# Retained values made with tokens on partitions, scores as weights, in a rearranged token stage

## What is computed

```python
Q = split_heads(x @ Wq); K = split_heads(x @ Wk); V = split_heads(x @ Wv)
G = jax.nn.swish(x @ Wg + bg)
Dmask = gammas[:, None, None] ** jnp.maximum(diff, 0.0) * causal
scores = jnp.einsum('bhtd,bhsd->bhts', Q, K) / scale
ret = jnp.einsum('bhts,bhsd->bhtd', scores * Dmask[None], V)
ret = ret.transpose(0, 2, 1, 3).reshape(B, T, D)
ln = (ret - mu) / jnp.sqrt(var + LN_EPS) * ln_gamma + ln_beta
return ln * G @ Wo + bo
```

## Time and profile before

| | before |
|---|---|
| median of 3 runs | 776.42 us (776.38 to 776.57) |
| profiled execution, its own time | 773.9 us |
| its span (first to last instruction) | 772.1 us |
| PE busy, PEld busy | 741.4, 608.0 us |
| DVE, ACT, POOL busy | 408.4, 325.5, 184.0 us |
| token stage, from the first q product to the end | from 515.4 us |

### The profile page before, as it was taken

The page is one execution under the profiler, slowest core; times in us unless marked ns, Lnnn a source line. Parts: engine busy times, 40 slices in busy tenths (PEclk is TensorE's granted clock), DMA queues, the critical chain, the costliest instruction groups (busy, mean ns, idle before and its releaser), DMA issues.

```text
span 772.1 us, 18699 instructions
## 1 busy us (share of the span) xinstructions
PE 741.4 (96%) x7464; PEld 608.0 (79%) x7464; DVE 408.4 (53%) x1100; ACT 325.5 (42%) x698; POOL 184.0 (24%) x150
## 2 busy tenths in 40 slices
PE   3999999999999999999999999999999999999985
PEld 2778888888888888988888888778777777777742
DVE  6433333334655534453523333494588788778685
ACT  2436555463353434444344445542343343343232
POOL 1510000003975664754600000011110110110010
PEclk9999999999999999999999999999999999999999
DMA  7141334331322123022121115260000000000001
GB/s 257 70 175 61 112 116 139 111 106 68 115 86 89 58 85 116 31 85 61 31 61 31 33 60 203 73 232 1 1 1 14 14 0 14 14 0 14 0 1 41
DMA packets 33956, 53.63 MB, mean 69 GB/s; under 512 B 2416, under 2 KB 23152, under 8 KB 32656
## 3 DMA queue, kind: packets, MB, share of 16 engines
q1 hardware_dynamic: 29168, 36.05, 14.1%
q0 software_dynamic: 3328, 16.78, 6.1%
q10 hardware_dynamic: 1440, 0.53, 0.3%
HBM read 51.19 MB, written 2.16 MB: 69 GB/s over the span
## 4 chain that ended last, share of the span: by engine, by line
PE 94%; DVE 4%; ACT 1%; issue 1%; DMA 1%; POOL 0%; DVEq 0%; POOLq 0%
PE bank L227 68%; PE bank L550 4%; PE bank L395 4%; PE bank L566 4%; PE bank L409 3%; PE bank L515 3%; PE bank L386 3%; PE bank L503 2%; PE bank L491 1%; PE bank L559 1%; DMA X<-in_x 1%; PE bank L465 1%; PE bank L522 0%; DVE h_max L1221 0%; PE bank L354 0%
## 5 line engine op out<-in xcount | busy, mean ns | idle before, releaser
L227 PE MATMUL bank<-ctx_high,wk_high 128*128 128x258 f32 x512 | 147.6, 288 | 0.0
L227 PE MATMUL bank<-ctx_low,wk_high 128*128 128x258 f32 x512 | 144.8, 283 | 0.0
L227 PE MATMUL bank<-ctx_high,wk_low 128*128 128x258 f32 x512 | 144.3, 282 | 0.0
L227 PEld LDWEIGHTS bank<-ctx_high,wk_high 128*128 128x128 f32 x512 | 96.9, 189 | 13.6 <-issue 13.3
L227 PE MATMUL bank<-wv_high,ctx_high 128*128 128x512 f32 x256 | 106.0, 414 | 0.0
L227 PE MATMUL bank<-wv_low,ctx_high 128*128 128x512 f32 x256 | 101.3, 396 | 0.0
L227 PE MATMUL bank<-wv_high,ctx_low 128*128 128x512 f32 x256 | 100.9, 394 | 0.0
L687 ACT ACTIVATE vals<-bank 128x512 f32<-128x512 f32 x64 | 38.2, 597 | 144.3 <-PE bank L227 144.3
L227 PEld LDWEIGHTS bank<-ctx_low,wk_high 128*128 128x128 f32 x512 | 96.8, 189 | 0.0
L227 PEld LDWEIGHTS bank<-ctx_high,wk_low 128*128 128x128 f32 x512 | 96.6, 189 | 0.0
L677 ACT ACTIVATE kT<-bank,bxk 128x257 f32<-128x257 f32 x128 | 60.1, 470 | 57.4 <-PE bank L227 57.2
(11 more groups left out here) (200 smaller groups left out, 1409.4 us busy)
## 6 DMA issues: line engine op xcount, KB each, us to landing
raw<-in_ctx_t SPq DMA_DIRECT2D x32, 514.0 KB, 4.0
stage<-in_w POOLq DMA_DIRECT2D x16, 1024.0 KB, 5.9
X<-in_x SPq DMA_DIRECT2D x4, 512.0 KB, 7.2
v_last<-last_values SPq DMA_DIRECT2D x32, 64.0 KB
out<-X SPq DMA_DIRECT2D x8, 256.0 KB, 2.0
stage<-in_w_xq SPq DMA_DIRECT2D x1, 1024.0 KB, 8.1
stage<-in_w_xk SPq DMA_DIRECT2D x1, 1024.0 KB, 13.2
stage<-in_w_xv SPq DMA_DIRECT2D x1, 1024.0 KB, 5.6
```

What stands on the lines that cost most here:

```text
L227: last = pe.matmul(to, left(i, c), right(j, c), start=(c == 0 and i + j == 0), stop=(c == C - 1 and i == 1))
```

## The change

`retain` swaps its operands: the decayed scores (128 rows, 128 columns) are the weights, the head's values are 32 moving columns, and the result has tokens on the partitions, as the normalisation wants it. `turn_retained`, ScalarE's copy into `rT_sb` and the tile itself are gone. `retention_scores` runs with g outside and j inside, and stands ahead of `feed_down`; it waits for the v product's copy and for `keep_hidden` at its start. TensorE waits for all four decays before the first half of `feed_up`, and `retain` comes behind that half. On VectorE `add_retained` and the moments of y come ahead of the scaling of the next tokens, `gate(t)` comes behind the whole of `quantise_tokens`, and `decay_scores` ahead of `add_forward` and `finish_gate`. On GpSimd the deviation of y comes ahead of `add_bias`.

```diff
-            def retention_scores(t):
+            def retention_scores(t, down, more):
 
                 pe.wait_ge(tqT_kept, t + 1)
                 pe.wait_ge(tkT_kept, t + 1)
-                for j in range(HG):
-                    if j == 2:
-                        pe.wait_ge(qkv_kept, 3 * t + 3)
-                    rows = slice(DH * j, DH * (j + 1))
-                    for g in range(C):
+                pe.wait_ge(qkv_kept, 3 * t + 3)
+                if down and more:
+                    pe.wait_ge(hT_kept, 2 * (t - 2) + 2)
+                for g in range(C):
+                    for j in range(HG):
+                        rows = slice(DH * j, DH * (j + 1))
                         last = pe.matmul(bank[S_BANK[j]][:, g * P:(g + 1) * P], tkT[rows, g, :], tqT[rows, g, :],
                                          start=True, stop=True)
-                    last.then_inc(s_ready, 1)
+                        if g == C - 1:
+                            last.then_inc(s_ready, 1)
...
-                for j in range(HG):
-                    pe.wait_ge(s_decayed, 4 * t + j + 1)
-                    for g in range(C):
+                for g in range(C):
+                    for j in range(HG):
                         h = HG * g + j
-                        last = pe.matmul(bank[7][DH * j:DH * (j + 1), g * P:(g + 1) * P],
-                                         v_sb[:, h * DH:(h + 1) * DH], s_sb[:, j, g, :], start=True, stop=True)
+                        last = pe.matmul(bank[7][:, h * DH:(h + 1) * DH], s_sb[:, j, g, :],
+                                         v_sb[:, h * DH:(h + 1) * DH], start=True, stop=True)
                 last.then_inc(retained, 1)
-
-            def turn_retained(t):
-                pe.wait_ge(rT_kept, t + 1)
-                for c in range(C):
-                    last = pe.transpose(bank[7][:, c * P:(c + 1) * P], rT_sb[:, c, :], idf[:, :])
-                last.then_inc(r_turned, 1)
...
                 project_tokens(t, 3, down)
+                retention_scores(t, down, more)
                 if down and more:
                     feed_down(t - 2)
-                retention_scores(t)
                 if more:
                     turn_tokens(t + 1)
                 if back:
                     turn_quantised(t - 1)
-                retain(t, 0 if not down else t - 1 if more else t - 2)
+                pe.wait_ge(s_decayed, 4 * t + 4)
                 if back:
                     feed_up(t - 1, (0, 1))
-                turn_retained(t)
+                retain(t, 0 if not down else t - 1 if more else t - 2)
                 if back:
                     feed_up(t - 1, (2, 3))
...
-                act.wait_ge(retained, t + 1)
-                act.activation(rT_sb[:, :, :], bank[7][:, :].rearrange("p (g n) -> p g n", g=C), ACT.Copy).then_inc(rT_kept, 1)
...
+                invert_deviation(y_norm, eps_ln, 1, t, y_moments, y_veps, y_rstd, t - 1)
                 add_bias(t + 1)
-                invert_deviation(y_norm, eps_ln, 1, t, y_moments, y_veps, y_rstd, t - 1)
...
-                dve.wait_ge(r_turned, t + 1)
+                dve.wait_ge(retained, t + 1)
...
                 if more:
-                    normalise_tokens(t + 1)
+                    measure_tokens(t + 1)
                 if back:
                     add_retained(t - 1, 4)
-                    quantise_tokens(t - 1, lambda: gate(t))
-                else:
-                    gate(t)
+                    measure_normed(t - 1)
+                if more:
+                    scale_tokens(t + 1)
+                if back:
+                    quantise_tokens(t - 1)
+                gate(t)
+                decay_scores(t)
                 if down and more:
                     add_forward(t - 2)
                 finish_gate(t)
-                decay_scores(t)
                 if more:
                     tokens_low(t + 1)
```

More of the change, by code:

```diff
@@ L146, in build_block @@
             sb(f"row_{n}", [D], F32, R + 64 * K + 2 * K * m) for m, n in enumerate(("gamma", "beta", "bg", "bo", "b2")))
-        tn, rT_sb = sb("tn", [D], F32, R + 40 * K), sb("rT_sb", [C, P], F32, R + 40 * K)
+        tn = sb("tn", [D], F32, R + 40 * K)
         tT = pair("tT", [C, P], R + 42 * K)
@@ L193, in build_block @@
         s_ready, s_decayed, retained = sem("s_ready"), sem("s_decayed"), sem("retained")
-        rT_kept, r_turned = sem("rT_kept"), sem("r_turned")
         r_stats, r_moments, r_veps, r_rstd = sem("r_stats"), sem("r_moments"), sem("r_veps"), sem("r_rstd")
@@ L1108, in moments_of, with measure_tokens, scale_tokens @@
                 dve.bn_aggr(norm[1][:, 0, :], norm[0][:, 0, :]).then_inc(moments, 1)
-            def normalise_tokens(t, between=None):
+            def measure_tokens(t):
                 moments_of(tile(t), t_norm, t_stats, t_moments, t + 1, 4)
-                if between:
-                    between()
+            def scale_tokens(t):
                 dve.wait_ge(t_rstd, t + 1)
@@ L1157, in _ @@
             dve.wait_ge(OT_kept, B)
-            normalise_tokens(0, lambda: output_low(3))
+            measure_tokens(0)
+            output_low(3)
+            scale_tokens(0)
             add_output(3)
@@ L1178, in quantiser, with measure_normed, quantise_tokens @@
                 dve.wait_ge(step, 4 * n + 4)
-            def quantise_tokens(t, between=None):
+            def measure_normed(t):
                 moments_of(tile(t), y_norm, y_stats, y_moments, t + 1, 5)
-                if between:
-                    between()
+            def quantise_tokens(t):
                 dve.wait_ge(y_rstd, t + 1)
@@ L1332, in _ @@
             add_retained(T - 1, 1)
-            quantise_tokens(T - 1, lambda: quantise_hidden(T - 2, 1, last_quant))
+            measure_normed(T - 1)
+            quantise_hidden(T - 2, 1, last_quant)
+            quantise_tokens(T - 1)
             add_forward(T - 3, part=r_sb[:, :])
```

## The result

The changed kernel took 797.6 us (median of 4 executions, 794.3 to 799.5) against 776.4 us (776.1 to 776.6): 1.027 times the time before, 95% interval 1.023 to 1.031. It was forecast slower, but 779.8 us and at most 788; it lost six times what the sum had.

The account below looks back on a forecast made before the run. TensorE, busy for 96% of the span, was taken to bound the kernel. Loop 0, tiles 0, 1 and 7 +0.4 + 0.6 - 0.4, clock falls +3.0, less 0.2: +3.4 on 776.4 gave 779.8 us, range 774.0 to 788.0.

Parts of the forecast that it names:

- Scores: Retention scores with j inside: four row groups run together, 1.1 us in place of 2.75, saving 1.65 a tile.
- Rival C: The scores' four row groups don't run together and stay at 2.75 us: +8.3, 788 us; chance 0.1.
- Retain: Retain with scores as weights: 32 loads at 0.111 us set the price, 3.55 us for 2.39, 1.16 more per tile.
- Rival D: A retain pair costs its short stream, not its load: retain 0.9 us, -21 in all, 759 us; chance 0.05.
- The wait for yqT: In the loop TensorE stands still before feed_up for ScalarE's copy to yqT: 0.9 us a tile (0.8 to 1.0).
- The sum of a loop turn: Tiles 2 to 6: -1.65 + 1.16 - 0.44 + 0.9 = -0.03 us each, within -3 and +4 over five.
- rival B: The sparse retain itself brings the clock down in most loop turns: 7.5 us on top, 787 us; chance 0.2.
- The price of one fall: A fall of TensorE's clock to half, as seen at tile 7's retain, costs 1.4 us, at most 1.65.
- the term of +3.0: One further fall to half clock in each of tiles 0 and 1, at 1.5 us each.
- VectorE in tile 1: In tile 1 no feed_down covers VectorE's quantise, gate and decays, which end at 554.4: cost +0.6 us.
- Tile 7: Quantise no longer waits for gate behind the g product: gain 0.4 us; the clock fall is in both kernels.
- The total: All terms together +3.4 us, with the median kept 2.5 above the profiled execution: 779.8 us.

Follow-up runs that it names:

- e1: The changed kernel with each retain matmul streaming up to 128 columns of values in place of 32: 782.3 us, 1.009 times the kernel before.
- e9: The changed kernel with streams of up to 64 columns in retain in place of 32: 788.3 us, 1.016 times the kernel before.
- e3: The kernel before with retain's operand swap alone, order untouched, j outside, without the turning back and its copy: 801.8 us, 1.033 times before.
- e2: The changed kernel, still 32 columns, with retain moved ahead of both halves of feed_up: 795.2 us.
- e5: The changed kernel with streams of up to 128 columns in retain, and retain ahead of both halves of feed_up: 779.2 us, 1.0045 times before.
- e6: e5 with GpSimd's add_bias moved behind the deviation of the retained values: 778.0 us, 1.0017 times the kernel before.
- run 32: Not a run: "run" is a verb here, in "run 32 pairs in 1.10 and 1.08 us", said of the scores and e7.
- e7: The changed kernel with retain ahead of feed_up, values as 32-column weights again and turned back, g outside, j inside: 764.9 us, 0.986 times before.

## Why the prediction was wrong

**Scores.** Right. 1.10 us, as forecast, from the pitch of 0.111 us in one row group and four groups at once. Rival C is out.

**Retain.** Right. 3.49 us for 3.55 forecast, 0.109 a pair. It stays 3.49 with 64 and 128 columns (e1, e9): the load is the price. Rival D is out.

**The wait for yqT.** Right. TensorE waits 1.04 us before feed_up for ScalarE (0.9 forecast).

```profile
596.78 1.89 PE L544 MATMUL bank<-w1q,yqT 128*128 128x512 bf16 x8 [1.04 <-ACT yqT L786]
```

**The sum of a loop turn.** Right at full clock: -0.03 forecast, +0.06 measured in e1 (29.47 for 29.41).

**The clock in the loop.** This is the step that failed first. The prediction named it (rival B) and gave it 2 in 10, "Against it: the fall at 727.3 came after work on only 32 rows and real waits, while retain works on all rows". Halves in tiles 2 to 6 were also its own sign of being wrong. e3 falls with no waits, e1 does not with them, and the only difference between e1 and the changed kernel is the length of the streams, with what they write over. That all rows work did not save it. The evidence was thin on both sides: nothing in the trace before had 32 loads of this width over streams this short, so nothing there spoke for a chance as low as 2 in 10.

The price of one fall was about right, 1.4 to 1.65 forecast: a turn of e2 is 30.7 us and one of e5, the same order at full clock, 29.0, so 1.7. That the loop's 7.2 us come so near to B's 7.5 is in part luck. Four of five turns have a fall in this execution; some 1.2 of the 7.2 are the tail of tile 1's half clock, which reaches 2.3 us into tile 2, and some 0.8 of tile 6's fall lie in tile 7 (estimates, half of the stretch). The four executions differ by 5 us, with mean granted clocks from 0.963 to 0.972.

**The clock in tiles 0, 1 and 7.** The step is the term of +3.0, one fall in tile 0 and one in tile 1 at 1.5 each, taken from the row with 3.3 us at 0.50. That the clock would fall there was right, the size was not. Tile 0 cost 1.5 in all, where 0.4 + 1.5 was forecast, but its half clock is twice as long as the row's and most of it lies behind the start of tile 1, at 536.6:

```profile
534.50:541.10 6.60, 6.60 (x22) 5.63 (x23) 3.07 (x6) 0.00 (x0) 0.74 (x2) 0.50 0.01 2
```

So this fall costs 3.3 us (an estimate, half of the stretch), of it 1.1 in tile 0 and 2.2 in tile 1. Without it tile 0 costs the forecast 0.4 (19.30 us in e1, 18.89 before). Tile 1 cost 10.0 instead of 0.6 + 1.5. At half clock its retain takes 6.67 us and not 3.49, and the clock stays down until behind the next feed_up:

```profile
560.36 3.19 PE bank L544 x7
563.55 6.67 PE bank L515 x32
570.22 3.41 PE bank L544 x8
573.63 6.31 PE bank L226 x24
```

That a fall prolongs itself in this way, by making the short streams last longer, fits the runs and is not shown apart: the half clock of tile 1 lasts 10.2 to 17.1 us in the three kernels with 32 columns, and 3.4 to 6.8 with 64 or 128. With wide streams of up to 128 columns (e1) the stretch is 6.6 us and not 16.8, and tile 1 costs 3.8 (30.2 for 26.4 us). So 6.2 of the 10.0 come from the short streams, the 2.2 from tile 0's fall among them, and 3.8 from the gap, the next point, and the fall that is left.

**VectorE in tile 1.** Costed at 0.6 without add_bias beside the scaling of y. "GpSimd does y's deviation ahead of add_bias: 1.3 us for a reader a turn later" looked only at who reads its result, not at what runs next to it. It puts 0.95 us on the path of the decays in tile 1, where nothing hides them.

**Tile 7.** Forecast -0.4 and no further fall, because its gap lies on that of the kernel before. The half clock now lies on feed_up and retain, and lasts 10.2 us in the changed kernel and 6.8 in e1, against 3.4 before: +5.5 and +2.4 with the end behind it. The end has half-clock stretches of its own in every run, before the change too; which part of the +5.5 is theirs was not separated.

**The total.** With the loop at rival B's 7.5, tile 0 at 1.5, tile 1 at 10.0 and the end at 5.5 the terms add up to 24.5 us, against 25.1 between the two profiled spans and 21.2 between the medians. The prediction kept the 2.5 us by which the median before stood above its profiled execution; after the change the profiled execution is the one above, by 1.5, so 4 of the 25.1 us are a matter of which execution was profiled. 788.0, the top of the range, held B but with the edge tiles at 1.5 each. The 0.9 us before the first change is not explained; q of tile 0 started between 515.2 and 516.9 us in the other runs, whatever they changed.

## What to carry to other kernels

When two forms of a product trade weights against moving columns, count the loads: with 32 moving columns the full-width load is the whole price here, and four narrow column groups side by side take a third of it (1.08 of 3.49 us, and 0.44 for turning back). Read the granted clock as well, for a queue that is busy by the rows can still lose TensorE its clock; if its streams are shorter than their loads, try wider ones: widening them under the load left the pair at 0.109 us and kept the clock up in the loop. Before moving work on GpSimd, look at what VectorE does at that moment.

## What the runs showed of the hardware

- The clock fell to half behind retain in pairs of a 0.109 us load and a 32-column stream, in 14 of 15 profiled loop turns (changed kernel, e2, e3), though TensorE was busy by the rows for 3.35 of the 3.40 us ahead of the fall in tile 2 of the changed kernel. With up to 64 or 128 columns in the same pairs it fell in none of 20 (e1, e5, e6, e9).
- Half clock lasted 3.4 us in the loop turns of the changed kernel, 3.4 or 6.8 in those of e3, and 17 us in tile 1, where retain itself ran in it.
- A float32 pair of a 128-column load and 32, 64 or 128 moving columns costs 0.109 us; four groups of 32 rows, or four of 32 columns, with the groups taken in turn, run 32 pairs in 1.10 and 1.08 us (the scores and e7).
- VectorE's tensor_scalar from SBUF to SBUF took 1.50 us beside a GpSimd addition that had started 0.07 us earlier, and 0.55 apart; the addition took 1.29 and 1.27.
